# Two causal attention stages of a hybrid network, rewritten around strips of 32 partitions

## The reference

```python
# rotary attention: 16 heads of 8 features
q, k, v = split(x @ W_qkv.T)
q, k = apply_rope(q), apply_rope(k)
scores = where(causal, q @ k.T / sqrt(8), -inf)
out = (softmax(scores) @ v) @ W_out.T

# latent attention: 8 query heads, 2 key/value groups, latent width 32
q = x @ wq                      # 8 heads of 128
k = (x @ wk_down) @ wk_up       # per group, 32 -> 128
v = (x @ wv_down) @ wv_up
out = (softmax(where(causal, q @ k.T * 128**-0.5, min)) @ v) @ wo
```

## Time and profile before

| | |
|---|---|
| median of 3 runs | 1947.14 us (1944.35 to 1948.87) |
| span of the profiled execution | 1933.1 us |
| mean granted TensorE clock | 0.888 |
| TensorE, VectorE busy | 1601.7, 1180.5 us |
| ScalarE, GpSimd busy | 786.5, 818.4 us |

### The profile page before, as it was taken

The page is one execution under the profiler, slowest core; times in us unless marked ns, Lnnn a source line. Parts: engine busy times, 40 slices in busy tenths (PEclk is TensorE's granted clock), DMA queues, the critical chain, the costliest instruction groups (busy, mean ns, idle before and its releaser), DMA issues.

```text
span 1933.1 us, 25832 instructions
## 1 busy us (share of the span) xinstructions
PE 1601.7 (83%) x8863; PEld 807.4 (42%) x8863; DVE 1180.5 (61%) x2315; ACT 786.5 (41%) x1031; POOL 818.4 (42%) x987
## 2 busy tenths in 40 slices
PE   4766699758999899999799789989545898988779
PEld 2222466412333333332466567766212333333256
DVE  5887633578788787883333333342355878897951
ACT  2222233343565565667333344444212343334433
POOL 2224646464554635455463644000001577456900
PEclk8788699867999999999799999979656898889979
DMA  4000000151000303000000000000143000000000
GB/s 139 1 0 0 1 1 0 59 121 29 2 2 12 41 3 51 2 2 1 1 1 0 0 1 0 0 1 0 49 117 96 1 1 1 1 1 1 1 1 22
DMA packets 31585, 36.86 MB, mean 19 GB/s; under 512 B 8606, under 2 KB 24703, under 8 KB 31362
## 3 DMA queue, kind: packets, MB, share of 16 engines
q1 hardware_dynamic: 27906, 29.29, 6.4%
q10 hardware_dynamic: 3520, 6.29, 1.6%
q0 software_dynamic: 64, 0.00, 0.0%
HBM read 26.10 MB, written 8.91 MB: 18 GB/s over the span
## 4 chain that ended last, share of the span: by engine, by line
PE 61%; DVE 16%; DMA 7%; SPq 3%; issue 2%; ACT 2%; ACTq 0%; DVEq 0%
PE PS L943 9%; PE PS L1355 9%; PE PS L931 9%; PE PS L1304 8%; PE PS L1374 8%; DVE sb_latent_acc L1462 3%; DMA sb_rope_K<-rope_parts 3%; PE PS L1723 3%; PE PS L1741 3%; SPq L1629 2%; DVE sb_latent_mp L1538 2%; DMA latent_parts<-sb_latent_parts 2%; DVE sb_rope_mp L1538 2%; DVE sb_latent_rec L1568 1%; PE PS L1735 1%
## 5 line engine op out<-in xcount | busy, mean ns | idle before, releaser
L1538 DVE TENSOR_REDUCE sb_rope_mp<-PS 128x1 f32<-128x512 f32 (+3 forms) x560 | 345.0, 669 | 76.5 <-PE PS L1308 36.9
L1418 ACT ACTIVATE sb_rope_PT<-PS 128x1024 f32<-128x1024 f32 (+3 forms) x320 | 273.3, 895 | 223.0 <-PE PS L1359 121.7
L1462 POOL TENSOR_TENSOR sb_latent_acc<-sb_latent_acc,sb_latent_PT 128x1536 f32<-128x1536 f32 (+3 forms) x72 | 223.2, 3101 | 72.4 <-ACT sb_latent_PT L1418 68.8
L1418 ACT ACTIVATE sb_latent_PT<-PS 128x1024 f32<-128x1024 f32 (+3 forms) x160 | 140.2, 895 | 243.3 <-PE PS L1359 80.9
L995 DVE SCALAR_TENSOR_TENSOR sb_X<-PS,sb_gates,sb_X 128x128 f32 (+1 forms) x320 | 90.1, 344 | 241.3 <-PE PS L943 241.2
L1304 PE MATMUL PS<-sb_rope_K,sb_rope_Q 96*128 96x512 bf16 (+3 forms) x640 | 211.7, 371 | 30.2 <-ACT sb_rope_V L1399 18.3
L1538 DVE TENSOR_REDUCE sb_latent_mp<-PS 128x1 f32<-128x512 f32 (+3 forms) x280 | 174.3, 666 | 46.2 <-PE PS L1304 32.5
L576 POOL TENSOR_SCALAR sb_pbelow<-sb_pa,sb_ptrial 128x512 f32<-128x512 f32 x124 | 197.0, 1599 | 6.4
L583 POOL TENSOR_TENSOR sb_pbelow<-sb_pbelow 128x1024 f32<-128x1024 f32 (+1 forms) x248 | 181.7, 733 | 19.6
L931 PE MATMUL PS<-sb_HT,sb_w 128*128 (+1 forms) x384 | 182.3, 612 | 3.6 <-DVE sb_seed L514 1.9
L1355 PE MATMUL PS<-sb_rope_Q,sb_rope_K 99*128 99x512 bf16 (+3 forms) x640 | 179.4, 352 | 1.4 <-ACT sb_rope_PT L1418 0.9
(11 more groups left out here) (291 smaller groups left out, 2438.7 us busy)
## 6 DMA issues: line engine op xcount, KB each, us to landing
latent_parts<-sb_latent_parts SPq DMA_DIRECT2D x36, 128.0 KB
sb_rope_Q<-rope_parts SPq DMA_DIRECT2D x9, 384.0 KB
rope_parts<-sb_rope_parts SPq DMA_DIRECT2D x24, 128.0 KB, 2.4
sb_rope_tab<-in_rotation SPq DMA_DIRECT2D x1, 2048.0 KB, 8.6
sb_rope_K<-rope_parts SPq DMA_DIRECT2D x6, 256.0 KB
sb_latent_Q<-latent_parts ACTq DMA_DIRECT2D x2, 768.0 KB
sb_latent_Q<-latent_parts SPq DMA_DIRECT2D x1, 1536.0 KB, 19.1
sb_rope_Q<-rope_parts ACTq DMA_DIRECT2D x6, 192.0 KB
```

Source lines behind the costliest of these rows:

```text
L1418: s.activation(self.PT[:, u % 2, 2 * p:2 * p + 2, q0:CH], k.PS[:, 2 * p:2 * p + 2, q0:CH], ACT.Exp, scale=self.scale).then_inc(self.exps[p ...
L1462: eng.tensor_tensor(acc, acc, new, ALU.add).then_inc(self.added[who], 1)
L1538: v.tensor_reduce(self.mp[:, n % 2, kc, heads[0]:heads[-1] + 1, i], k.PS[:, bank, 0:len(heads) * w].rearrange("p (h k) -> p h k", h=len(he ...
```

## The change

`CausalHeads` is no longer used. A class `Strips` with the subclasses `RopeStrips` and `LatentStrips` takes its place. Nothing goes through DRAM.

- Head j of a quad lies on partitions 32j to 32j+31, its strip. Matmuls contract over one strip, so heads use different row strips of the array.
- Rotary: the bf16 parts stay in SBUF. "select" matmuls with 0/1 matrices (`select`, loaded as a new input of 384 KB) arrange them into `QA`, `KA`, `QB`, `KB`; a score or a maximum is two bf16 matmuls of 32 rows. The negated maxima go into spare rows of `QB` (as `QN`) by matmuls and a ScalarE copy, not by DMAs.
- Latent: `Q` and `K` stay fp32 on 32 partitions; a score is a bf16 matmul of three rows (the negated maximum) and one fp32 matmul. GpSimd adds the weights of all four heads in two units of three; in the third, matmuls with ones sum them ("part"). The split of the maxima moves to GpSimd.
- The opening works on sets of four banks, two halves by turns. The first maxima of the first two chunks are reduced four heads at a time ("quad"); all others singly.
- The loop's order becomes: scores of two heads beside two maxima in the other two strips, weighted sum of the unit before, scores of the other two heads beside two maxima, further items. Sequences are ordered by chunk: 0, 0, 1, 2, then all of 3, then the rest downwards. The weights have three buffers, not two.
- The constants get one more matrix and column; the next layer norm's left-over statistics follow the last chunk.

```diff
+class Strips(Stage):
+    tiles_ahead = NT - TPC
+    R = 3
+    AHEAD = 3
+    PTS = 3
...
+    def chunk_maxima(self, n):
+        c, g = self.seq[n]
+        return [("max", n, i, kc, j) for i in range(TPC) for kc in range(c + 1) for j in (2, 3, 0, 1)]
...
+            want = max([np.ceil((d - done) / max(1, at - u) / 2) * 2 for at, d, _ in due if d > done] or [0])
...
+            pairs = (0, 1) if not mine or mine[0][4] == 2 else (1, 0)
+            if u < total:
+                plan.append((u, f"scores{pairs[0]}"))
+                plan += ring(mine[0:2])
+            if 1 <= u <= total:
+                plan.append((u - 1, "weighted"))
+            if u < total:
+                plan.append((u, f"scores{pairs[1]}"))
+                plan += ring(mine[2:4])
+            plan += self.beside(u)
+            plan += [(u, it) for it in relays[u]]
+            plan += ring(mine[4:])
...
+        if u:
+            pe.wait_ge(self.exps[p], u)
+        diag = kj >= c * TPC
+        pair = (2 * p, 2 * p + 1)
+        if diag:
+            for j in pair:
+                pe.matmul(k.PS[:, j, q0:q0 + P], k.identb[:, :], k.mask_kq[:, :], start=True, stop=False,
+                          skip_group_check=True)
+        self.pe_max_masks(pe, beside)
+        for j in pair:
+            ins = self.pe_head(pe, j, n, kj, q0, not diag)
+        ins.then_inc(self.scores[p], 1)
+        self.pe_maxima(pe, beside)
...
+    def pe_max_masks(self, pe, items):
+        k = self.k
+        for ring, (_, n, i, kc, j) in items:
+            b, uses = self.bank_of(ring)
+            if uses:
+                pe.wait_ge(self.ring_free[b], uses)
...
+class RopeStrips(Strips):
...
+        plan.append(new(("project", 0)))
+        step("rotate", 0)
+        plan.append(new(("values", 0)))
+        plan.append(new(("project", 1)))
+        step("rotate", 1)
+        step("split", 0)
+        selects(0, "QA", "KA", "QB", "KB")
+        plan.append(new(("project", 2)))
+        step("rotate", 2)
+        quads(0)
+        step("split", 1)
+        selects(1, "QA", "KA", "QB", "KB")
...
+        pe.matmul(k.PS[:, j, q0:CH], self.KA[strip, g, kj * P:(kj + 1) * P],
+                  self.QA[strip, g, c * CH + q0:(c + 1) * CH], start=start, stop=False, skip_group_check=True)
+        return pe.matmul(k.PS[:, j, q0:CH], self.KB[strip, g, kj * P:(kj + 1) * P], self.QN[strip, n % 2, q0:CH],
+                         start=False, stop=True, skip_group_check=True)
...
+class LatentStrips(Strips):
...
+    def pe_sums(self, kj):
+        return kj % 3 == 0
...
+        pe.matmul(k.PS[:, j, q0:CH], k.onesb[rows, :], self.negT[rows, n % 2, q0:CH], start=start, stop=False,
+                  skip_group_check=True)
+        return pe.matmul(k.PS[:, j, q0:CH], self.K[strip, g, kj * P:(kj + 1) * P],
+                         self.Q[strip, g, c * CH + q0:(c + 1) * CH], start=False, stop=True, skip_group_check=True)
...
@@ def rope_attention():
-            a = CausalHeads(k, "rope", ln, 4, [(k.wqkvT[:, i, :], k.wqkvT[:, 3 + i, :]) for i in range(2)],
-                            blocks, 96, 4, k.wqkvT[:, 2, :], 16, 8, float(8 ** -0.5), k.woutT,
-                            d["rope_parts"], True, False, 4.0)
+            a = RopeStrips(k, "rope", ln, [(k.wqkvT[:, i, :], k.wqkvT[:, 3 + i, :]) for i in range(2)],
+                           k.wqkvT[:, 2, :], k.woutT, d["rotation"])
@@ def latent_attention():
-            a = CausalHeads(k, "latent", ln, 2, sources + [(k.wkv[:, :, :].rearrange("p a l -> p (a l)"), None)], (qb, kb), 96, 1,
-                            k.wkv[:, 1, :], 2, 32, float(P ** -0.5), k.wy, d["latent_parts"], False, True, 4.5)
+            a = LatentStrips(k, "latent", ln, k.wc, k.wkrep, k.wkv[:, 1, :], k.wy)
```

More of the change, by code:

```diff
@@ L37, with left_tiles @@
     tiles_ahead = 0
+    def left_tiles(self):
+        return self.tiles_ahead, NT - self.tiles_ahead
     def sync(self, sp):
@@ L105, in __init__ @@
         self.eps = sb("eps", [P, 1])
+        self.select = sb("select", [P, len(RopeStrips.PATTERNS), P], BF16)
+        self.neg_rows = self.cst[:, CST_ORDER + 8:CST_ORDER + 9]
         self.PS = ctx.enter_context(nc.psum_tensor("PS", [P, 8, CH], F32))
@@ L116, in bank @@
         return self.PS[:, b, 0:cols]
-N_CST = 5 + 8 + 2
+N_CST = 5 + 8 + 2 + 1
 class NormMemory:
@@ L191, in __init__ @@
         self.ready = self.mem.ready
-        self.ahead = 0
+        self.left = (0, NT)
     def statistics(self, v, n, tiles):
@@ L212, in vector @@
                 v.wait_ge(sem, val)
-        self.statistics(v, self.ahead, NT - self.ahead)
+        self.statistics(v, *self.left)
         for n in range(NT):
-            v.wait_ge(m.steps, first + n + 1)
+            v.wait_ge(m.steps, first + (n + 1 if self.left[0] + self.left[1] == NT else NT))
             ins = v.bn_aggr(m.mv[:, n, :], m.stats[:, n, :])
@@ L291, in __init__ @@
         k.wy = sb("wy", [P, 2, P])
+        k.wkrep = sb("wkrep", [P, 2, 4, 32])
         self.n_zeroed = 5
@@ L307, in alloc @@
         self.wo = sb("wo", [P, 8, P])
+        self.selection = sb("selection", [P, len(RopeStrips.PATTERNS), P])
         self.row0 = sb("row0", [3, 8, P])
@@ L355, in loads @@
         load(k.wkv[:, 1, :], d["L1_attn_b_wv_down"])
+        load(self.selection[:, :, :], d["selection"])
         return early, out
@@ L440, in gpsimd @@
         g.tensor_copy(k.identb[:, :], k.ident).then_inc(self.ready, 1)
+        g.tensor_copy(k.select[:, :, :], s.selection[:, :, :]).then_inc(self.ready, 1)
         g.tensor_copy(k.mask_qk[:, :], k.cst[:, (5 + 8) * P:(6 + 8) * P]).then_inc(self.ready, 1)
         g.tensor_copy(k.mask_kq[:, :], k.cst[:, (6 + 8) * P:(7 + 8) * P]).then_inc(self.ready, 1)
+        for i in range(2):
+            g.tensor_copy(k.wkrep[:, i, :, :], k.wkv[:, 0, 32 * i:32 * i + 32].rearrange("p (a l) -> p a l", a=1)
+                          .broadcast_to([P, 4, 32])).then_inc(self.ready, 1)
     def tensor(self, pe):
@@ L1863 @@
 CST_ORDER = N_CST * P
-CST_COLS = N_CST * P + 8
+CST_COLS = N_CST * P + 9
 def constants():
@@ L1881, in constants, with selection @@
     c[:, 14 * P:15 * P] = np.where(r[:, None] > r[None, :], MASKED, 0.0)
-    c[:, CST_ORDER:] = 8 - np.arange(8)
+    c[:, 15 * P:16 * P] = (r[:, None] // 32 == r[None, :] // 32) & (r[:, None] % 32 == 0)
+    c[:, CST_ORDER:CST_ORDER + 8] = 8 - np.arange(8)
+    c[:, CST_ORDER + 8] = (r % 32 >= RopeStrips.NEG_ROW) & (r % 32 < RopeStrips.NEG_ROW + 3)
+    return c
+def selection():
+    c = np.zeros((P, len(RopeStrips.PATTERNS), P), np.float32)
+    r = np.arange(P)
+    for i, blocks in enumerate(RopeStrips.PATTERNS):
+        for b in blocks:
+            c[r, i, 32 * (r % 32 // 8) + 8 * b + r % 8] = 1.0
     return c
@@ L1917, in norm @@
                 if producer.tiles_ahead:
-                    producer.next_ln, ln.ahead = ln, producer.tiles_ahead
+                    producer.next_ln, ln.left = ln, producer.left_tiles()
                     break
@@ L2053 @@
     arrays["in_rotation"] = rotation()
+    arrays["in_selection"] = selection()
     d = {n[3:]: nc.dram_tensor(n, a.shape, F32, kind="ExternalInput").ap() for n, a in arrays.items()}
```

728 lines of the change are left out of this document (722 added, 6 removed).

## The result

The changed kernel takes **2117.9 us** (median of 3 runs, 2112.2 to 2117.95) against 1947.1: ratio 1.0892, 95% interval 1.0834 to 1.095. The forecast was slower at 1994, with a range up to 2095: the direction was right, and 124 us of the loss were not foreseen. Single executions of one kernel differ by up to 2.7% here (2075.4 to 2131.7 us in a version of run 3), so parts of a loop are compared within traces and totals by their intervals.

The account below looks back on a forecast made before the run. The prediction took the old rotary loop as TensorE-bound at 2.9 us a unit. From 1947.1 us it added setup 0.5, rotary opening 14, rotary loop 50, latent opening -60.5, latent loop 41, tail 2: 1994 us, range 1885 to 2095.

Parts of the forecast that it names:

- Rotary opening: Projections to first maxima before the rotary loop: 86 us removed, 100 us new with cold matmuls, so +14.
- Rotary loop, four maxima: Rotary units with four maxima: ring waits close a cycle through the weighted sum, 2.87 us per full unit; whole loop 518, +50.
- Six maxima: 21 rotary units carry six maxima, four banks deep: 4.1 us per full unit, 4.05 per diagonal one.
- Two maxima or none: Rotary units, 24 with two maxima and 7 with none: full ones 2.74 us each, diagonal ones shorter.
- the exponentials' own cycle: Rotary loop: weighted sum, first matmul, exponential and hand-overs in turn, 2.74 us a unit.
- Rival C: The clock falls in the rotary loop because TensorE idles 40% of a cycle: loop 575, total 2051 us; chance 0.09.
- Latent opening: Projections and first maxima before the latent loop: 110.5 us removed, 50 new, so -60.5; the DMA wait goes.
- Latent loop: Latent unit loop: 363 us removed, 372 new, divided by 0.92 for the clock to 404, so +41.
- D: Both loops: maxima don't close the cycle because banks come free earlier; total 1907 us, faster; chance 0.27.
- B: Both loops: row strips overlap incompletely, starting one weight load apart, 144 us on top: 2138; chance 0.14.
- S: Both loops: row strips don't overlap at all, 940 us on top: 2934; chance 0.03.
- P: Rotary stage gains so much that GpSimd's perturbation search bounds, at most 73 us gained before the experts: 1809; chance 0.02.

Follow-up runs that it names:

- run 3: Changed kernel, ring-bank waits moved behind the scores: 1.1305; or taken one bank at a time: 1.0944 alone, 1.0758 with the weighted sum after both score phases.
- run 2: Changed kernel with the unit order scores, scores, weighted sum of the unit before, in place of scores, weighted sum, scores: ratio 1.0769 to the kernel before.
- run 1: Changed kernel plus eight matmuls of zeros before each weighted sum's wait for exponentials: 1.1187 at full width, 1.094 in the two-column control.
- run 6: Changed kernel plus three rounds of zero matmuls ahead of the third pair of maxima in units with six: ratio 1.0826 to the kernel before.
- run 5: Changed kernel with every unit beginning with heads 0 and 1: 1.0587, 2051.0 us; sums last too: 1.0666; latent half with both edits under the old rotary stage: 0.995.
- latent_only: Rotary stage of the kernel before, latent stage of the changed kernel: 1960.6 us, ratio 1.0099.
- fill_six: The kernel of run 6, with zero matmuls only ahead of third pairs of maxima: ratio 1.0826.
- run 7: Changed kernel, heads 0 and 1 first, plus sums last in thin units and six-maxima filler: 1.0411 (old rotary stage 0.982); or plus single ring waits: 1.0486, 1.0433 with late sums.

## Why the prediction was right or wrong

- **Rotary opening**, forecast 100: 93 at clock 0.62. Right, and cold as assumed.
- **Rotary loop, four maxima.** The prediction's 76 x 2.87 and 88 for the diagonal units, with a share of 31 for masks, turns and outputs (my split of its 53), make 337; measured 385. The mechanism was right, though the ring closes a second cycle of the same length (run 2), and the cycle was too short, 3.07: +0.20 x 108 = 22, of which 0.08 is the hand-over from VectorE, taken as 0.06 from a ScalarE row and measured at 0.14, and 0.10 the score phase. The other 26 us I read from the lengths of the units without a test of its own: the four diagonal units of a long sequence take 15.0 with their turn, where the forecast had 13.1, and the units with the normaliser and the output 3.73 and 3.67. Others ran at half clock (4.77 for 3.07); run 1 puts the clock in this part at up to 23 us. How the 26 divide stays open.
- **Six maxima.** "21 carry six maxima (four banks deep: 4.1)": 92 with their share, measured 120. Two mis-sizes: the pair's own cycle (three pairs at 1.54 are 4.6), and the clock, which run 6 puts at 14 us.
- **Two maxima or none.** This is the step that failed as reasoning. The prediction took "the exponentials' own cycle", 2.74, for these units, which holds only if each pair of heads keeps its place in the unit. The diff it quotes has the line that makes the places alternate. 89 with their share, measured 118; run 5's edit gives 89. That the two 89 agree is partly luck: with the edit a steady unit with two maxima takes 2.89, not 2.74, and other units less.
- **The clock of the rotary loop.** The sum has no factor for it, so it keeps the 0.99 of before; measured 0.84 over the loop. Rival C named it, at 0.87 and for 57 us, but as a cause in itself. Runs 1 and 5 show that in the last part it followed from the alternation, run 6 that in the first part it is a cost of its own. The Trainium skill, "TensorE: Matmul & The Clock Gate", "A second HAM failure mode: psum-queue depth-cycling", says that short idle times between groups of matmuls, as PSUM banks are cycled, make the clock oscillate; the trace agrees (0.50 and 1.00 in units that follow each other), and I had not weighed it.
- **Latent opening**, forecast 50: 34. The mechanism was right. It ran warm (0.95), where the prediction took cold matmuls.
- **Latent loop.** 404 forecast, 451 measured. By parts (its classes divided by its 0.92, and a share of the other terms): 132 and 149, 161 and 153, 110 and 149. Its sums are 1 us too high each: the terms give 204 and 131, not 205 and 132. In the middle two errors cancel: without the division the forecast is 148, and 153 were measured at clock 0.99. The last part is the alternation again, 33 us by run 5. But that counts clock too: the same code took 132 in `latent_only` and in `fill_six`, which leave the alternation in, at clock 0.83, not 0.71, and against those run 5's 116 is 16 less. Of the first part's 17 us the clock is 10 by run 6; the other 7 stay open.
- **Rivals.** D, that the maxima don't close the cycle: no, 3.07 a unit. B, row strips that overlap incompletely: no. S, no overlap: no. P: no, the rotary stage gained nothing. The range failed at its upper end because the clock and the cycle were separate rivals, and here they came together; the alternation was among none of them.

Where the loss itself comes from: TensorE's work in a rotary unit fell, but before, the loop had no wait to speak of (445 busy of 468; in steady units of 2.82 none at all), and it now runs at the pace of a ring of three banks: units of 3.07, with TensorE busy 76% of their time (the row from 750 to 768 in the last section). A longer ring was not tried; banks 0 to 7 are all in use.

```profile
686.00:704.00 18.00, 18.00 (x148) 7.76 (x146) 15.44 (x25) 11.09 (x15) 11.48 (x16) 1.00 0.01 2
```

Even repaired (554 and 567 us in run 7) it stays above 468. The latent stage had more to gain, its opening alone 77 us.

## What to carry to other kernels

Where TensorE's work is cut in a loop that it filled, first write the cycle through every ring and every pair of buffers, with hand-overs from rows of the same engine pair, and do it for each class of unit that the planner can make, its thin ones too. A plan that sorts work by what it meets can change the order from one unit to the next; look for it in the code, not in the steady part of the trace. And price such a loop at both clock levels: a wait costs its own time, and more when the clock falls with it (3.52 became 5.34 here).

## What the runs showed of the hardware

- TensorE was granted 0.50 in units where it was busy 4.84 of 6.60 and 5.48 of 6.70 us, and 1.00 in the steady units, busy 13.74 of 18.00, a share between those two:

```profile
750.00:768.00 18.00, 13.74 (x150) 3.02 (x142) 14.23 (x23) 11.83 (x12) 14.59 (x23) 1.00 0.00 1
```

  So the busy share of a stretch did not tell its clock. The same latent code took 149, 153 and 149 us behind the new rotary stage (clock 0.87, 0.99, 0.71) and 159, 153 and 132 behind the old one (0.79, 0.99, 0.83).
- Small VectorE operations beside GpSimd's search ended only when its additions did. At a turn, in the timeline and then in GpSimd's groups by form:

```profile
850.65 4.51 POOL L597 TENSOR_TENSOR sb_pbelow<-sb_pbelow 128x1024 f32<-128x1024 f32 x3
...
852.28 0.76 DVE L1949 CAST sb_rope_negp<-sb_rope_neg 128x16 bf16<-128x16 f32 x1
853.08 1.29 DVE L1950 TENSOR_TENSOR sb_rope_rest<-sb_rope_neg,sb_rope_negp 128x16 f32<-128x16 f32 x1
854.40 0.20 DVE L1951 CAST sb_rope_negp<-sb_rope_rest 128x16 bf16<-128x16 f32 x1
```

```profile
L597 POOL TENSOR_TENSOR sb_pbelow<-sb_pbelow 128x1024 f32<-128x1024 f32 x31 | 72.8, 2350 | 2.6
L597 POOL TENSOR_TENSOR sb_pbelow<-sb_pbelow 128x512 f32<-128x512 f32 x31 | 39.3, 1268 | 2.4
```

  GpSimd's first addition ends near 853.0, its second near 854.3. VectorE's cast ends at 853.04 (the next one, at 854.40, takes 0.20), and its subtraction, begun with the second addition, at 854.37. So each lasted until GpSimd's instruction was over. The Trainium skill's "GPSIMD Engine Reference" ("1. Specifications", the row "SBUF interfaces") says that the two share their SBUF interfaces, and that VectorE instructions with two inputs in SBUF contend there. The trace agrees for the subtraction, which has two; the cast has one. This turn's unit took 9.24 us. No experiment was made of it, so the cause is not shown.
